# Attention and expert layer on one core: inter-chunk matmuls before the next quad's state step, dense and wide groups alternated, state sums a quad later

## What is computed

```python
x  = L0_attn_x                                  # (8, 1024, 128)
xn = layernorm(x)                               # over the last axis, no affine
# linear attention, 16 heads of 8, in causal chunks of 64 tokens
q, k, v = split(xn @ W_qkv);  k = layernorm(k)  # per head
for each chunk:
    inter = S @ q_c                             # state of all chunks before
    intra = causal_mask(q_c @ k_c.T) @ v_c
    S     = S + v_c.T @ k_c                     # per head 8 x 8
    y_c   = inter + intra
attn = y @ W_o
# mixture of 8 experts, one expert per token
e   = argmax(xn @ centroids.T)
h   = relu((layernorm(xn) * g[e] + b[e]) @ w1[e].T + b1[e])
ffn = xn + sigmoid(xn @ centroids[e]) * (h @ w2[e].T + b2[e])
return x + attn + ffn
```

## Time and profile before

| | us |
|---|---|
| median of 3 runs (lowest to highest) | 363.81 (362.58 to 365.19) |
| the profiled execution, its own time | 363.22 |
| its span, from first to last instruction | 361.4 |
| TensorE busy (share of the span) | 341.2 (94%) |
| VectorE, GpSimd, ScalarE busy | 283.6 (78%), 250.2 (69%), 241.7 (67%) |

### The profile page before, as it was taken

The page is one execution under the profiler, slowest core; times in us unless marked ns, Lnnn a source line. Parts: engine busy times, 40 slices in busy tenths (PEclk is TensorE's granted clock), DMA queues, the critical chain, the costliest instruction groups (busy, mean ns, idle before and its releaser), DMA issues. The chain is left out here.

```text
span 361.4 us, 17478 instructions
## 1 busy us (share of the span) xinstructions
PE 341.2 (94%) x6868; PEld 293.5 (81%) x6868; DVE 283.6 (78%) x799; ACT 241.7 (67%) x657; POOL 250.2 (69%) x245
## 2 busy tenths in 40 slices
PE   7799999989899999999999989999999999999990
PEld 7466776777587787777877878999999999999990
DVE  8887898898785988977878786788887778877760
ACT  4788677777667657666665735766677667766660
POOL 3388567889886865455455503888887888888884
PEclk9999999999999999999999999999999999999996
DMA  7403213021433233255233225555555555555420
GB/s 203 103 22 92 63 38 86 26 77 54 128 98 92 91 93 91 82 149 152 93 99 100 78 58 137 69 72 72 68 64 77 72 76 67 70 75 61 37 23 0
DMA packets 46705, 28.99 MB, mean 80 GB/s; under 512 B 5096, under 2 KB 44320, under 8 KB 46624
## 3 DMA queue, kind: packets, MB, share of 16 engines
q1 hardware_dynamic: 34352, 19.34, 19.6%
q0 software_dynamic: 12272, 8.54, 17.1%
HBM read 14.53 MB, written 13.78 MB: 78 GB/s over the span
## 5 line engine op out<-in xcount | busy, mean ns | idle before, releaser
L495 POOL DMA_INDIRECT out_dram<-qx,rows x71 | 112.7, 1588 | 36.0 <-issue 21.9
L695 ACT ACTIVATE qx<-sc,b1T 128x128 f32<-128x128 f32 x280 | 79.8, 368 | 40.4 <-PE sc L1424 40.4
L421 POOL DMA_INDIRECT slots_d<-rows,pos_i x64 | 62.8, 981 | 41.3 <-PE bank L1331 10.7
L857 DVE TENSOR_TENSOR pr<-sc,causal 128x1536 f32<-128x1536 f32 (+2 forms) x33 | 63.5, 1926 | 16.3 <-PE sc L1277 16.2
L1432 PE MATMUL bank<-tokens,qx 128*128 128x128 f32 x568 | 75.2, 276 | 0.7 <-ACT qx L695 0.7
L1424 PE MATMUL sc<-wide,tokens 128*128 128x128 f32 x560 | 74.1, 275 | 0.4 <-issue 0.4
L1432 PEld LDWEIGHTS bank<-tokens,qx 128*128 128x128 f32 x568 | 69.0, 192 | 1.1 <-ACT qx L695 1.1
L1424 PEld LDWEIGHTS sc<-wide,tokens 128*128 128x128 f32 x560 | 68.2, 192 | 0.6 <-issue 0.6
L1016 DVE COPY tokens<-xT 128x1024 f32 x71 | 53.3, 752 | 0.2 <-issue 0.2
L1277 PEld LDWEIGHTS sc<-qx,kT 32*64 32x64 f32 x2048 | 32.9, 130 | 16.8 <-issue 16.4
L1031 DVE SCALAR_TENSOR_TENSOR qx<-bank,rows,qx 128x128 f32<-128x128 f32 x71 | 24.8, 350 | 27.2 <-PE bank L1432 26.5
(11 more groups left out here) (167 smaller groups left out, 531.4 us busy)
## 6 DMA issues: line engine op xcount, KB each, us to landing
rows<-slots_d SPq DMA_DIRECT2D x71, 66.0 KB, 2.0
out_dram<-tokens SPq DMA_DIRECT2D x16, 256.0 KB, 2.7
tokens<-in_L_attn_x_dram SPq DMA_DIRECT2D x7, 512.0 KB, 4.2
w1raw<-in_L_ffn_w_dram SPq DMA_DIRECT2D x8, 256.0 KB, 3.3
w2raw<-in_L_ffn_w_dram SPq DMA_DIRECT2D x8, 256.0 KB, 2.9
out_dram<-qx,rows POOLq DMA_INDIRECT x71, 3.4
slots_d<-rows,pos_i POOLq DMA_INDIRECT x64
slots_d<-empty SPq DMA_DIRECT2D x9, 66.0 KB
```

The source lines that it names most:

```text
L421: pool.indirect_dma_start(slots_d, bass.IndirectOffsetOnAxis(ap=pos_i[:, t:t + 1], axis=0), rows[:, t, :], None)\
L495: pool.indirect_dma_start(out_rows, bass.IndirectOffsetOnAxis(ap=xs[:, a, D + 2:D + 3].bitcast(U32), axis=0), ye[:, a, :], None, bounds_ch ...
L695: last = nc.scalar.activation(ht[:, k % 2, c * P:(c + 1) * P], inner(k)[:, c * P:(c + 1) * P], ACT.Relu, bias=b1T[:, bass.ds(e * FC + c, 1)])
L857: nc.vector.tensor_tensor(pr[:, h % 2, a:G, w].rearrange("p g (j t) -> p g j t", t=CH), sc[:, a * BANK:G * BANK].rearrange("p (g w) -> p g ...
```

## The change

It does five things.

1. `inter_first(n - 1)` and `inter_second(n - 1)` stand right behind `kT_project(n + 1)` and ahead of `state_step(n)`; before they stood in quad n, behind it. They now add to what `products` began (`start` moves to the first product).
2. The groups of a quad are ordered so that `scores` and `products` each have a wide group on both sides. The only dense groups in a row are `inter_first`, `inter_second`, `state_step`, all in 64x64 tiles.
3. The banks are laid out so that the two halves of a state step lie in neighbouring banks, and one instruction (`dstates`, 128x512) takes both. `q_project(n + 1)` waits for it, now with `k_transpose` alone between itself and the state step. In quads 3, 5, 7 and 9 it waits for `ranks` too, which stands behind `dstates`.
4. The sum after the second chunk (`state_end`) is made a quad later, for n - 1 right before `state_middle(n)`; `dstate` has two copies.
5. VectorE scales the values ahead of the odd half's `score_mask`, not behind it. The last `b1_fold` moves from quad 15 to the end of the even half of quad 14 and writes its products to a scratch tile, so that it waits for the weight load and not for the transpose. `se_scale(0)` and `(1)` stand ahead of `se_weights`. The last `send_rows` are one quad half sooner: none is left for quad 15.

The core of the diff (renumbered and unchanged lines left out):

```diff
-        banks = [ctx.enter_context(nc.psum_tensor(f"bank{i}", [P, BANK], F32)) for i in range(4)]
-        FA, FB, Y = banks[0], banks[1], banks[2:4]
+        bank = ctx.enter_context(nc.psum_tensor("bank", [P, 4 * BANK], F32))
+        banks = [bank[:, i * BANK:(i + 1) * BANK] for i in range(4)]
+        Y, FA, FB = (banks[0], banks[2]), banks[1], banks[3]
...
@@ vector
-            def dstate_first(n):
+            def dstates(n):
                 dve.wait_ge(s("ds_ps"), n + 1)
-                reach(dve, s("smid_ready"), n)
-                nc.vector.tensor_tensor(dstate[:, 0, :, :], Y[n % 2][:, 0:HALF * GW].rearrange("p (i k) -> p i k", k=GW),
-                                        bcast(smask[:, :], 1, HALF), ALU.mult).then_inc(s("dsta_sb"), 1)
-
-            def dstate_second(n):
-                reach(dve, s("state_ready"), n)
-                nc.vector.tensor_tensor(dstate[:, 1, :, :], FA[:, 0:HALF * GW].rearrange("p (i k) -> p i k", k=GW),
-                                        bcast(smask[:, :], 1, HALF), ALU.mult).then_inc(s("dstb_sb"), 1)
...
+                reach(dve, s("state_ready"), min(n - 1, NQ - 2))
+                reach(dve, s("smid_ready"), n - 1)
+                if n < NQ - 2:
...
+                    nc.vector.tensor_tensor(dstate[:, n % 2, :, :, :], pair, bcast(bcast(smask[:, :], 1, HALF), 1, NC),
+                                            ALU.mult).then_inc(s("dst_sb"), 1)
...
@@ vector, the last folds
+                    if n == NQ - 2:
+                        b1_fold(E - 1)
...
-                        b1_fold(E - 1)
-                        dstate_first(n)
-                        score_mask(h)
...
@@ tensor
             def q_project(n):
-                if n:
-                    pe.wait_ge(s("dstb_sb"), min(n, NQ - 2))
+                reach(pe, s("dst_sb"), n)
                 if n in (4, 6, 8, 10):
                     pe.wait_ge(s("rank_sb"), n // 2 - 1)
...
                 if h % 2 == 0:
                     if more:
                         kT_project(n + 1)
+                    if n:
+                        inter_first(n - 1)
+                        inter_second(n - 1)
                     state_step(n)
+                    if more:
+                        k_transpose(n + 1)
+                        q_project(n + 1)
                     if h:
                         products(h - 1)
-                    inter_first(n)
-                    if more:
-                        k_transpose(n + 1)
-                    if n and out_early(n):
-                        output(n - 1)
-                    if more:
-                        q_project(n + 1)
-                else:
-                    products(h - 1)
-                    if n < 8 and n % 2 == 1:
-                        affinities(n // 2)
                     if more:
                         v_project(n + 1, FB)
-                    inter_second(n)
-                    if n and not out_early(n):
+                else:
+                    if n:
                         output(n - 1)
+                    products(h - 1)
+                    if with_affinities(n):
+                        affinities(n // 2)
...
+            inter_first(NQ - 1)
+            inter_second(NQ - 1)
             products(NH - 1)
```

166 lines of the change are left out of this document (89 added, 77 removed).

## The result

| | us |
|---|---|
| before, median of 10 runs (lowest to highest) | 363.37 (362.32 to 365.19) |
| after, median of 10 runs | 367.34 (365.91 to 368.88) |
| ratio after / before, 95% interval | 1.0102 (1.0078 to 1.0126) |
| span of the profiled execution after | 365.2 (before 361.4) |

What follows compares the result with a forecast made beforehand. TensorE's chain of groups was taken to bound the attention part, GpSimd's adding DMAs the very end. Terms summed to -1.2 us from the profiled 363.2, giving 362.0; the forecast was set at 362.4, range 358.9 to 367.2.

Steps and rivals of the forecast that it cites:

- Holes, -3.6 predicted: TensorE's attention blocks: holes in dense runs vanish, -3.0 us, and half of a 1.2 us scores hole goes, -0.6.
- a block that has already used up the lead of its queue shows the seam: TensorE's stream: fixed grid points show as holes late in dense runs, not right behind wide groups; basis for -3.0 us.
- the holes have another cause: Rival on TensorE: holes come when a transfer is late, wherever the block stands; no -3.6 us gain, 366.0; chance 0.13.
- products and scores now have a wide group on both sides: TensorE's order: the reason given for holes in dense runs being gone, -3.0 us.
- `q_project`, +4.9 predicted: Quads 0 to 13: q_project waits 0.35 us each for the merged state-step copy, bounds 0.27 and 0.45.
- Ranks, +0.8 predicted: Quads 3, 5, 7, 9: q_project also waits for ranks behind dstates, taken at 0.2 us each.
- part 2: q_project's wait for the merged copy, 0.35 us in each of fourteen quads, +4.9 us.
- Parts 4 to 6, -2.4 predicted: Quads: inter_first waits vanish, -1.0 us; v_scale ahead of the second mask, -0.7; fewer tile shape changes, -0.7.
- The end, -0.9 predicted: Last quads: scores(31)'s mask wait goes, -0.7 us net of 0.4 given back; last scatters leave sooner, -0.2.
- the supply rival: Scores blocks on TensorE: instruction supply costs more than its holes, wide groups restore late blocks; 359.0 us, chance 0.20.
- if holes move into the scores blocks: TensorE's scores blocks: a stated condition under which the prediction would be wrong; no size given.
- The VectorE rival: Late quads and those with count: VectorE's queue becomes the bound, scores wait for the mask; +6, 368.4 us, chance 0.17.

Runs made afterwards that it cites:

- e3: Changed kernel with its 22 warming transposes cut into 44 of half the size, shifting TensorE's later instructions 44 places; ratio 1.0127 to the kernel before.
- e4: Kernel before with its 22 warming transposes cut into 44 of half the size, shifting TensorE's instruction grid 44 places; ratio 1.0044.
- e12: Changed kernel with odd products ahead of q_project, key root ahead of q_expand, folds of quads 8 to 13 behind the result, ten quad 0 transposes; 364.16 us, ratio 1.0019.
- e16: e12 plus five one-column memsets on VectorE behind the attention part; 362.11 us, ratio 0.9962 to the kernel before.
- e17: Changed kernel with four one-column memsets on VectorE behind the attention part, no fold moved, run once; span 367.2 us.
- e10: Changed kernel with the merged state-step copy split into two halves, q_project waiting for the first alone; 366.09 us, ratio 1.0071 to the kernel before.
- e1: Changed kernel with the odd half's products(h-1) moved between k_transpose and q_project on TensorE; 367.11 us, ratio 1.0082 to the kernel before.
- e6: Changed kernel with the move of e1, key root ahead of q_expand, and folds of quads 8 to 13 behind the result; 365.48 us, ratio 1.0060.
- e7: Changed kernel with ten identity transposes that nothing reads filling TensorE's idle time in quad 0; ratio 1.0061 to the kernel before.
- the two queue moves alone: Changed kernel with ScalarE's key root ahead of the first two q_expand and VectorE's folds of quads 8 to 13 behind the odd half's result; ratio 1.0179.
- e9: Changed kernel with VectorE's dstates and ranks ahead of ln_inverse and ln_shift; 373.57 us, ratio 1.0271 to the kernel before.

## Why the prediction was wrong, by its own steps

1. **Holes, -3.6 predicted, -0.36 measured.** This is the largest miss. The grid was right (e3, e4). Two steps failed. The first is the rule "a block that has already used up the lead of its queue shows the seam; right behind a wide group, where the queue had time to fill, it doesn't": 1.4 us came in scores(24), right behind two wide groups, and in e12 and e16 a block behind `k_transpose` had 0.58 and 1.89. What decides is when the transfer of queue 8 lands, so the mechanism is that of the rival "the holes have another cause", priced at 366.0, and I gave it 0.13. (The 55 transfers, which I took for those of all engines, match TensorE's stream alone.) The second is "products and scores now have a wide group on both sides": in quad 15 they haven't, as the order of the end shows, and 2.1 us of holes came there, for which the sum had no term. In quads 1 to 14, which it was about, the holes fell by 2.5. How much of that fall is the order and how much the place of the grid isn't shown: under the same order and the same grid scores(24) had 0.4 to 2.1 (e17, e10), and with the grid shifted the quads had almost none (e3).
2. **`q_project`, +4.9 predicted.** It waits in 14 quads as foreseen, 0.40 and not 0.35 in the ordinary ones, and its block costs another 0.10 behind the wait: 14 x 0.50 = 7.0, above my upper bound of 0.45 each. That is read from the rows; taking the wait away gave back only 0.18 in an early quad (e1).
3. **Ranks, +0.8 predicted.** The row L977 takes 0.27, near my 0.2. What I missed is that VectorE is late by then in just these quads, and that `ln_inverse` and `ln_shift` now stand ahead. With part 2 in them, the four quads lost 3.17. In quads 7 and 9 the other orders give that back (e12: 13.38 and 12.42, before 13.18 and 12.54); in 3 and 5 none did, and that VectorE's full queue is the reason there is argued from its rows, not shown by a run.
4. **Parts 4 to 6, -2.4 predicted.** Of the other ten quads nine pay 0.50 and quad 14 pays 0.2, 4.7 in all, and they lost 0.54, so by this difference the order without the wait gave them some 4.2, about 0.4 each, where I had 0.17. I had the sign right and the size at less than half. That e6 brings the late ones to 11.9 points the same way, though it moves the folds too.
5. **The end, -0.9 predicted, -0.55 measured** without the holes of step 1.
6. **Quad 0: not in the sum, +1.25**, 1.0 of it by the granted clock (e7, e10). Whether it falls there differs between executions of like kernels, so this term may be partly luck of the profiled one.

The sum by measured terms: -0.36 + 1.25 + 3.17 + 0.54 - 0.55 + 0.06 = 4.11, and 3.8 in the span. The misses of steps 1, 2, 3 and 6 add up; the larger gain of step 4 hid part of them. Of "what would show it", the wait in 14 quads, longest in 3 and 5, and no wait at scores(31) came out; "no products block over 1.15" failed at 214.50 (1.34) and in the two products blocks above. The late scores blocks took 1.28 and 1.50 in quad 11, on both sides of the 1.35 to 1.43 before: no sign of the supply rival. One thing that I named against myself, "if holes move into the scores blocks", is what happened in scores(24). The VectorE rival was not what the changed kernel paid (0.2 us of such waits), but it stood right behind, in VectorE's own work: e1 walked into it.

## What to carry to other kernels

A wait that is removed is worth what the next queue allows. Before an operand comes later, list what stands behind its readers on every engine, as the mask stood behind the fold and `v_scale`; e1 alone and the two queue moves alone gave 0.1 each in quads 8 to 14, and 2.7 together. This program has holes on a fixed grid, 1.6 to some 5 us in sum, so a comparison of two orders within 1% carries some 2 us of luck: count them in both traces, shift the stream by a few instructions, and compare without them. And read the granted clock wherever an engine first goes idle.

## What the runs showed of the hardware

- Holes of TensorE at every 256th instruction of its stream: most crossings cost nothing, a few 0.1 to 2.1 us. Place fixed by the program, size not (0.58 and 1.89 at one place). In 87 of 89 holes TensorE went on 1.2 to 1.6 us behind the end of a 16 KB transfer of queue 8.
- Behind an idle time of 1.84 us from such a hole (e10) the granted clock was 0.68 from 170 to 172 us and 0.64 from 172 to 175, part of it at the lower level of 1.2 GHz; that hole was paid twice. Behind an idle time of 1.67 (e16) it stayed at 1.00.
- The same two waits of 0.88 and 0.94 us in quad 0 were followed by a fall of the clock in the kernel after and by none in e6, e9 and e10.
- The alignment of VectorE's stream decided 1.9 us of an expert part of 133: four memsets of one column cost that, five gave it back in the other kernel. Which place of the stream matters, and why the scatters behind it stay slow, the runs leave open.
- A masked copy out of two neighbouring PSUM banks (128x512) took 0.69, the same as a copy out of one; half of it 0.41.
